# Layer norms of a two-block kernel: from VectorE's subtract-and-multiply to a row shift on VectorE and a scale-and-bias on ScalarE

## The chip, the cores and the metric

One core of a Trainium2 chip runs the kernel. The core has five engines, each with its own instruction queue worked off in order: PE (TensorE), DVE (VectorE), ACT (ScalarE), POOL (GpSimd) and SP (SyncE, which here only starts DMAs). They wait for each other through semaphores. The metric is the device time of one launch in microseconds, lower is better; the kernel before takes 7072.08 us in the median of 3 runs (7069.32 to 7072.81).

## The reference

A batch of 32 sequences of 256 tokens with 128 channels goes through two residual blocks. Cut to what matters:

```
_layernorm(x) = (x - mean(x)) / sqrt(var(x) + 1e-5)        # per token, over 128 channels

x = x + A(_layernorm(x))          # A: q, k, v with causal conv and silu, rope, a gated delta rule
                                  #    over 16 heads of 64, output gate, Wo
x = x + F(_layernorm(x)), where F(y):
    h = LN(y) * g1 + b1;  y = y + softmax_attention(h) @ Wo
    m = LN(y) * g2 + b2;  y + top-2-of-8 experts(m)
```

So there are four layer norms for each sequence: one of the input (`xn`), one of the first block's result (`xf`), one of `xf` again (`hn` for attention) and one of `x2`, the state behind attention (`hn` again, for the experts). Each is 256 tokens, held as two tiles of 128 tokens (partitions) by 128 channels.

## The kernel before

All five engines run the same software pipeline of turns. In turn i, `back` works on sequence i (the delta rule: heads, a blocked triangular inverse, state), `front` on sequence i+1 (norm, projections, conv, rope), `V` on i (values), `attn` on i-1 (output gate, second block's norms and attention, router) and `experts` on i-2. There are turns -1 to 32; turns 3 to 29 are one hardware loop. A hand-written table `SIDE` says after which milestone of `back` each engine takes which step of the other streams. A step that an engine has no part in costs it nothing, and each engine keeps to the table's order, so a step that waits holds up all that stands behind it on its engine.

The layer norms stand at these places:

- `front stat` at "start" and `front xln` at ("head", 2): statistics of `xin`, then `xn`. PE turns `xn` over at ("head", 3), step `xT`, ahead of expert step `up 1` and the next pair of heads. ACT's place at ("head", 2) lies behind `silu 0` and `silu 1` of the attention stream, which need POOL's `normalise`.
- `attn stat` and `attn xf` at ("head", 11): `x1` becomes `xf`, and the statistics of `xf` follow at once. `gate 0` of the front stands between them.
- `attn hT` at "kT": `xf` becomes `hn`, PE turns it over, ACT copies it to `hT` with g1 and b1.
- `attn fWo` at ("o", 0) has the statistics of `x2`; `attn mT` at "end" makes `hn`, PE turns it over, ACT copies it to `mT` with g2 and b2, and the router follows.

Each norm is made so: DVE takes bn_stats and bn_aggr (mean and variance in `mv` or `fmv`) and adds eps (`ln_stats`, L1408 to L1416); POOL raises the variance to -1/2 (`rstd` L711, `frstd` L789); DVE then makes `(x - mean) * rstd` by one tensor_scalar for each of the two tiles (`ln_apply`, L1421). `v_ln` and `f_ln` are the semaphores that count these DVE steps, 5 for each norm. POOL's `normalise` (L721, L723) multiplies the delta rule's output of one token tile, 128x1024, in two instructions; its second tile is done in the next turn at ("head", 1), its first in "cross" 1.

Of the kernel before, what the change touches and what calls it, by code (L numbers as in the profile page):

```python
# [27 lines left out]
ALU = mybir.AluOpType  # L28
# [3 lines left out]
P = 128  # L32
# [182 lines left out]
def program(nc, a, out):  # L215
# [3 lines left out]
    with ExitStack() as ctx:  # L219
        def sb(name, shape, dt=F32):  # L220
            return ctx.enter_context(nc.sbuf_tensor(name, shape, dt))
# [46 lines left out]
        def bank(use):  # L268
            return banks[bank_of[use]]
# [190 lines left out]
        x1_ready = signal("x1_ready", 1)  # L460
        v_ln = signal("v_ln", 5)
        p_rstd = signal("p_rstd", 1)
# [45 lines left out]
        a_yT = signal("a_yT", 4)  # L508
        f_ln = signal("f_ln", 15)
        fp_rstd = signal("fp_rstd", 3)  # L510
# [124 lines left out]
        def _(sp):  # L635
# [19 lines left out]
            def one(i):  # L655
# [21 lines left out]
                if ahead is not None and not (last and ahead == B - 1):  # L677
                    hold(v_ln.sem, v_ln.at(ahead, 5))
                    sp.dma_start(xin[:], x_rows(i[0] + 2 if isinstance(i, tuple) else ahead + 1)).then_inc(x_in.sem, 16)
# [15 lines left out]
        def _(pool):  # L695
# [87 lines left out]
            def attn(j, step, n):  # L783

                if step == "norm":
                    normalise(j, 1)
                elif step in ("stat", "xf", "fWo"):
                    pool.wait_ge(f_ln.sem, f_ln.at(j, {"stat": 3, "xf": 8, "fWo": 13}[step]))
                    g.tensor_tensor(frstd[:], fmv[:, :, 1], neg_half[:, 0:1].to_broadcast([P, NT]),  # L789
                                    ALU.pow).then_inc(fp_rstd.sem, 1)  # L790
                elif step == "b2":

                    g.tensor_tensor(x1[:], x1[:], x2[:], ALU.add).then_inc(p_xs.sem, 1)
# [35 lines left out]
        def _(act):  # L829
# [36 lines left out]
            def values(i, step, m):  # L866
# [17 lines left out]
                elif step == "copy":  # L884
                    act.wait_ge(*full_at(i, ("vT", m)))
                    if m == 0 and begun(i, 0):
                        act.wait_ge(v_y.sem, v_y.at(i, 0))
                    s.copy(V[:, :, 4 * m:4 * m + 4, :],  # L888
                           bank(("vT", m))[:].rearrange("p (t h d) -> p t h d", t=NT, h=4)).then_inc(a_V.sem, 1)

            def front(k, step, n):
                if step == "xT":
                    act.wait_ge(*full_at(k, "xT"))
# [85 lines left out]
            def attn(j, step, n):  # L979
# [55 lines left out]
        def _(pe):  # L1035
# [54 lines left out]
            def front(k, step, n):  # L1090
                if step == "xT":
                    pe.wait_ge(v_ln.sem, v_ln.at(k, 5))
                    wait_free(pe, "xT")
# [166 lines left out]
            def attn(j, step, n):  # L1260
# [20 lines left out]
                elif step == "hT":  # L1281
                    pe.wait_ge(f_ln.sem, f_ln.at(j, 10))
                    for t in range(NT):
# [66 lines left out]
                elif step == "mT":  # L1350
                    pe.wait_ge(f_ln.sem, f_ln.at(j, 15))
                    for t in range(NT):
# [44 lines left out]
        def _(dve):  # L1397
# [19 lines left out]

            def ln_apply(i, x_, mv_, rs, out_, sig, rsig, rk):
                dve.wait_ge(rsig.sem, rsig.at(i, rk))
                for t in range(NT):  # L1420
                    v.tensor_scalar(out_[:, t, :], x_[:, t, :], mv_[:, t, 0:1], rs[:, t:t + 1], ALU.subtract,  # L1421
                                    ALU.mult).then_inc(sig.sem, 1)

# [95 lines left out]
            def front(k, step, n):  # L1519
# [3 lines left out]
                elif step == "xln":  # L1523
                    ln_apply(k, xin, mv, rstd, xn, v_ln, p_rstd, 1)
                elif step == "gate" and n == 0:
# [121 lines left out]
            def attn(j, step, n):  # L1647
# [12 lines left out]
                elif step == "xf":  # L1660
                    ln_apply(j, x1, fmv, frstd, xf, f_ln, fp_rstd, 1)
                    dve.wait_ge(f_ln.sem, f_ln.at(j, 5))
                    ln_stats(j, xf, fstats, fmv, f_ln, 5)
                elif step == "hT":
                    ln_apply(j, xf, fmv, frstd, hn, f_ln, fp_rstd, 2)
                elif step == "fqk":
# [43 lines left out]
                elif step == "fWo":  # L1710
# [126 lines left out]
```

## Time and profile before

| | |
|---|---|
| median of 3 runs | 7072.08 us |
| profiled execution, first to last instruction | 7067.6 us |
| PE busy | 5137.7 us (73%) |
| DVE busy | 4870.4 us (69%) |
| ACT busy | 3485.1 us (49%) |
| POOL busy | 2615.7 us (37%) |
| chain that ended last | PE 41%, issue 23%, DVE 19%, ACT 10%, POOL 6% |

The profile page gives for the profiled execution its span, from the first to the last instruction; the median of the timed runs lies 4.5 us above it, which is what lies around the span. No engine is busy all the time: the table says what each engine had to do, the chain says whose work the end waited for, and here it goes back and forth between engines, so where an instruction stands in its turn matters more than how much its engine has to do.

### The profile page before, as it was taken

To read this page: it belongs to the slowest core of one execution; us is meant where nothing else is said; L and a number is where in the kernel's file an instruction comes from. 1 tells how busy PE (TensorE), PEld (TensorE's weight loads), DVE (VectorE), ACT (ScalarE), POOL (GpSimd) and SP (SyncE) were. 2 spreads that over 40 slices of the span, in tenths; PEclk is the share of its full clock that TensorE was granted. 3 is DMA by queue.
4 is the path that set the end of the run, shared out by engine and by line. 5 is a ranking of instruction groups with operands and counts; after the bars stand their busy time and mean duration, and the time that the engine had idled before them with its cause. 6 is when DMAs were issued, how large, how long until landed. Compare 5 with 4: busy or idle time off the path is not lost.

```text
span 7067.6 us, 126933 instructions
## 1 busy us (share of the span) xinstructions
PE 5137.7 (73%) x40448; PEld 3663.3 (52%) x40448; DVE 4870.4 (69%) x11585; ACT 3485.1 (49%) x5995; POOL 2615.7 (37%) x2957
## 2 busy tenths in 40 slices
PE   3677777777767777777777677777777777777776
PEld 2455555555545555555555455555455454555555
DVE  5667777667776677776677776677766777767752
ACT  2345554545554545545555545455444555455533
POOL 3444333344333444333443334343333433334420
PEclk6677877777877878777778778777777787777777
DMA  1000010000010100110000101000100001000001
GB/s 47 8 20 25 24 34 30 28 26 27 27 34 27 31 22 24 34 34 24 28 25 27 34 27 31 25 28 26 34 27 28 25 24 34 30 28 28 25 25 44
DMA packets 214675, 199.48 MB, mean 28 GB/s; under 512 B 13848, under 2 KB 176416, under 8 KB 209696
## 3 DMA queue, kind: packets, MB, share of 16 engines
q1 hardware_dynamic: 213920, 190.01, 8.9%
q8 instruction: 401, 6.57, 0.4%
q14 instruction: 354, 2.90, 0.1%
HBM read 148.02 MB, written 4.19 MB: 22 GB/s over the span
## 4 chain that ended last, share of the span: by engine, by line
PE 41%; issue 23%; DVE 19%; ACT 10%; POOL 6%; DVEq 1%; ACTq 0%; DMA 0%; SPq 0%; POOLq 0%
PE bank L1039 38%; DVE acc L1433 3%; PE bank L1043 3%; DVE NP L1575 3%; DVE tmpb L1602 2%; DVE mx L1684 2%; DVE Gam L1566 2%; ACT acc L854 2%; POOL fo L716 1%; ACT h L1026 1%; ACT L883 1%; POOL QK L816 1%; POOL nrm L728 1%; DVE Gam L1605 1%; ACT acc L877 1%
## 5 line engine op out<-in xcount | busy, mean ns | idle before, releaser
L1039 PE MATMUL bank<-QK 64*128 64x256 f32 (+1 forms) x4096 | 858.2, 427 | 628.9 <-DVE NP L1575 298.3
L1433 DVE SCALAR_TENSOR_TENSOR acc<-bank,conv_w,acc 128x255 f32<-128x255 f32 (+2 forms) x2304 | 931.8, 473 | 379.7 <-ACT acc L854 197.5
L1039 PEld LDWEIGHTS bank<-QK 64*128 64x128 f32 (+1 forms) x4096 | 358.1, 173 | 1059.4 <-issue 378.1
L1026 ACT ACTIVATE h<-bank,b 128x256 f32<-128x256 f32 x1024 | 415.8, 473 | 611.2 <-PE bank L1039 607.5
L854 ACT ACTIVATE acc<-bank,conv_b,conv_w 128x256 f32<-128x256 f32 x512 | 260.8, 559 | 868.6 <-PE bank L1039 716.3
L1039 PE MATMUL bank<-mT,W 128*128 128x256 f32 x2048 | 665.5, 483 | 24.4 <-DMA W<-in_W 22.6
L789 POOL TENSOR_TENSOR frstd<-fmv,neg_half 128x2 f32<-128x2 f32 x96 | 66.8, 696 | 1350.7 <-DVE fmv L1416 1350.7
L1039 PEld LDWEIGHTS bank<-mT,W 128*128 128x128 f32 x2048 | 502.2, 255 | 121.1 <-DMA W<-in_W 24.1
L1039 PE MATMUL bank<-W,h 128*128 128x128 f32 x4096 | 515.7, 280 | 55.4 <-DVE QK L1701 51.4
L810 POOL TENSOR_TENSOR sq<-acc 128x256 f32<-128x256 f32 x256 | 186.4, 728 | 973.7 <-ACT acc L860 973.7
L1039 PEld LDWEIGHTS bank<-W,h 128*128 128x128 f32 x4096 | 490.9, 194 | 105.6 <-DVE QK L1701 63.0
L1566 DVE TENSOR_TENSOR_SCAN Gam<-bank,ident_pad 128x258 f32<-128x258 f32 x512 | 351.8, 687 | 272.5 <-PE bank L1039 272.5
L746 POOL TENSOR_TENSOR Gam<-Gam 128x80 f32<-128x80 f32 (+11 forms) x736 | 272.3, 370 | 549.3 <-DVE Gam L1597 501.5
L924 ACT COPY Gam<-NP 32x256 f32<-32x256 f32 x512 | 321.6, 628 | 306.3 <-DVE fac L1582 301.8
L818 POOL TENSOR_TENSOR rot<-rot,sin 128x512 f32<-128x512 f32 x256 | 384.2, 1501 | 153.6 <-DVE rot L1549 153.6
L1039 PE MATMUL bank<-xnT,Wqkv 128*128 128x256 f32 x1024 | 381.1, 508 | 72.1 <-DVE acc L1433 71.9
L1575 DVE SCALAR_TENSOR_TENSOR NP<-bank,es,Gam 128x256 f32<-128x256 f32 x1024 | 432.9, 466 | 0.0
L1605 DVE TENSOR_TENSOR Gam<-Gam,tmpb 128x112 f32<-128x112 f32 (+29 forms) x992 | 368.3, 371 | 38.8 <-DVE tmpb L1602 5.7
L800 POOL TENSOR_TENSOR V<-V,nrm 128x1024 f32<-128x1024 f32 x64 | 121.4, 1918 | 735.1 <-ACT V L888 735.1
L1684 DVE TENSOR_REDUCE mx<-bank 128x2 f32<-128x512 f32 x512 | 319.7, 679 | 80.5 <-PE bank L1039 80.5
L1602 DVE TENSOR_TENSOR tmpb<-Gam 128x112 f32<-128x112 f32 (+29 forms) x992 | 352.7, 356 | 23.4
L1002 ACT ACTIVATE pT<-bank 128x512 f32<-128x512 f32 x512 | 281.8, 596 | 90.5 <-PE bank L1039 89.6
(227 smaller groups left out, 11769.9 us busy)
## 6 DMA issues: line engine op xcount, KB each, us to landing
W<-in_W SPq DMA_DIRECT2D x512, 256.0 KB, 2.9
QK<-QK SPq DMA_DIRECT2D x32, 1024.0 KB, 5.4
xin<-in_x SPq DMA_DIRECT2D x32, 128.0 KB, 2.2
x<-in_x SPq DMA_DIRECT2D x32, 128.0 KB, 2.2
xnG<-xnT SPq DMA_DIRECT2D x32, 128.0 KB, 2.0
out<-moe SPq DMA_DIRECT2D x32, 128.0 KB, 2.0
NP<-in_c_alpha_sel SPq DMA_DIRECT2D x1, 1024.0 KB, 5.0
Wqkv<-in_Wq SPq DMA_DIRECT2D x1, 512.0 KB, 6.1
```

Of the source, the lines that this page charges most:

```text
L818: g.tensor_tensor(rot[:, b], rot[:, b], sin[:].unsqueeze(1).to_broadcast([P, 2, T]), ALU.mult).then_inc(p_rope.sem, 1)
L854: ins = s.activation(acc[:, n % 2, kind, :], ps[:, kind, :], ACT.Identity, bias=conv_b[:, kind, n:n + 1], scale=conv_w[:, kind, n, PAD:KT])
L924: ins = s.copy(Dg[ROWS[q]].rearrange("p k (t h) -> p k t h", t=NT)[:, :, :, heads - 4:heads], units[:, :, :, heads - 4:heads])
L1002: s.activation(pT[:, n % 4], pair(bank(("st", n))), ACT.Exp, scale=float(FD) ** -0.5)\
L1026: ins = s.activation(h1[:, n % 2, f, :], ps[:, q, :], ACT.Gelu_apprx_tanh, bias=b1[:, n, f:f + 1])
L1039: return mm(out_, lhsT, rhs, start=first, stop=last)
L1433: v.scalar_tensor_tensor(acc[:, n % 2, m, j:T], ps[:, m, 0:T - j], conv_w[:, kind, c, PAD - j:KT - j], acc[:, n % 2, m, j:T], ALU.mult, AL ...
L1566: v.tensor_tensor_scan(Gam[:, h, :], ps[:, 0:NT * GW], ident_pad[:], 0.0, ALU.mult, ALU.add)\
L1575: ins = v.scalar_tensor_tensor(NP[:, t * H + h - 1, :, :], ps[:, t * T:(t + 1) * T].rearrange("p (a k) -> p a k", a=2), es[:, t, h - 1:h], ...
L1602: v.tensor_tensor(tmp_, Eb[:, r + 1:, r:r + 1].to_broadcast([P, n, w]), X[:, r:r + 1, 0:w].to_broadcast([P, n, w]), ALU.mult).then_inc(v_b ...
L1605: v.tensor_tensor(X[:, r + 1:, 0:w], X[:, r + 1:, 0:w], tmp_, ALU.subtract).then_inc(v_blk.sem, 1)
L1684: v.tensor_reduce(mx[:, :, n], ps, AX.X, ALU.max).then_inc(v_mx.sem, 1)
```

## The change

The two tiles' subtract-and-multiply leaves DVE. In its place DVE makes one small tensor of two columns, `shift = -mean * rstd` (one scalar_tensor_tensor of 128x2), and ACT makes `x * rstd + shift`, one activation (Identity, scale and bias from columns) for each tile. Who needs the result waits for new semaphores of ACT, `a_xn` (1 a sequence) and `a_fln` (3 a sequence): PE before each of the three transposes, SP before it loads the next `xin`, and DVE itself before the statistics of `xf`. `v_ln` now counts 4 and `f_ln` 12 steps.

```diff
-            def ln_apply(i, x_, mv_, rs, out_, sig, rsig, rk):
+            def ln_shift(i, mv_, rs, shift_, sig, rsig, rk):
+
                 dve.wait_ge(rsig.sem, rsig.at(i, rk))
-                for t in range(NT):
-                    v.tensor_scalar(out_[:, t, :], x_[:, t, :], mv_[:, t, 0:1], rs[:, t:t + 1], ALU.subtract,
-                                    ALU.mult).then_inc(sig.sem, 1)
+                v.scalar_tensor_tensor(shift_[:], mv_[:, :, 0], -1.0, rs[:], ALU.mult, ALU.mult).then_inc(sig.sem, 1)
...
+            def apply(out_, x_, rs, shift_, done):
+
+                for t in range(NT):
+                    ins = s.activation(out_[:, t, :], x_[:, t, :], ACT.Identity, bias=shift_[:, t:t + 1],
+                                       scale=rs[:, t:t + 1])
+                ins.then_inc(done.sem, 1)
+
             def front(k, step, n):
-                if step == "xT":
+                if step == "xln":
+                    act.wait_ge(v_ln.sem, v_ln.at(k, 4))
+                    apply(xn, xin, rstd, shift, a_xn)
+                elif step == "xT":
...
+                elif step == "xf":
+                    act.wait_ge(f_ln.sem, f_ln.at(j, 4))
+                    apply(xf, x1, frstd, fshift, a_fln)
                 elif step == "hT":
+                    act.wait_ge(f_ln.sem, f_ln.at(j, 8))
+                    apply(hn, xf, frstd, fshift, a_fln)
                     act.wait_ge(*full_at(j, "hT"))
...
                 elif step == "mT":
+                    act.wait_ge(f_ln.sem, f_ln.at(j, 12))
+                    apply(hn, x2, frstd, fshift, a_fln)
                     act.wait_ge(*full_at(j, "mT"))
...
                 if step == "xT":
-                    pe.wait_ge(v_ln.sem, v_ln.at(k, 5))
+                    pe.wait_ge(a_xn.sem, a_xn.at(k, 1))
...
                 elif step == "hT":
-                    pe.wait_ge(f_ln.sem, f_ln.at(j, 10))
+                    pe.wait_ge(a_fln.sem, a_fln.at(j, 2))
...
                 elif step == "mT":
-                    pe.wait_ge(f_ln.sem, f_ln.at(j, 15))
+                    pe.wait_ge(a_fln.sem, a_fln.at(j, 3))
...
                 elif step == "xf":
-                    ln_apply(j, x1, fmv, frstd, xf, f_ln, fp_rstd, 1)
-                    dve.wait_ge(f_ln.sem, f_ln.at(j, 5))
-                    ln_stats(j, xf, fstats, fmv, f_ln, 5)
+                    ln_shift(j, fmv, frstd, fshift, f_ln, fp_rstd, 1)
+                    dve.wait_ge(a_fln.sem, a_fln.at(j, 1))
+                    ln_stats(j, xf, fstats, fmv, f_ln, 4)
```

The other calls of `ln_apply` (steps `xln`, `hT` and `mT`) become `ln_shift` in the same way, and POOL's three waits for `f_ln` count 3, 7 and 11 in place of 3, 8 and 13.

On ACT, in the hardware loop from "end" over the loop's branch to ("head", 3), the order before is this (L1011 is the copy to `mT`, L1026 the experts' gelu, L982 `silu 0` and `silu 1`, L896 the copy of the turned `xn`):

```order
L1011 ACTIVATE mT<-bank,ln_gb 128x256
L1015 ACT_TABLE_LOAD
L1015 ACTIVATE ex<-lg 128x16
L910 COPY sumsT<-bank 96x256
L557 REGISTER_ALU
L557 COMPARE_AND_BRANCH
L1026 ACT_TABLE_LOAD
L1026 ACTIVATE h<-bank,b 128x256 x4
L982 ACT_TABLE_LOAD
L982 ACTIVATE Gam<-Gam 128x1024
L982 ACTIVATE Kt<-Kt 128x1024
L896 COPY xnT<-bank 128x256
```

The same place now (lines are numbered anew: L898 is `apply`, L996 the two silu):

```order
L898 ACTIVATE hn<-x,fshift,frstd 128x128 x2
L1031 REGISTER_ALU
L1032 ACTIVATE mT<-bank,ln_gb 128x256
L1036 ACT_TABLE_LOAD
...
L1047 ACTIVATE h<-bank,b 128x256 x4
L996 ACT_TABLE_LOAD
L996 ACTIVATE Gam<-Gam 128x1024
L996 ACTIVATE Kt<-Kt 128x1024
L898 ACTIVATE xn<-xin,shift,rstd 128x128 x2
L910 COPY xnT<-bank 128x256
```

The pair of `hn` stands directly ahead of the copy to `mT`, the pair of `xn` behind both silu; no table load has come in.

On DVE at ("head", 11), the order before, from the end of `gate 0` (L1533) over `xf` and its statistics to the experts' sum (L1766):

```order
L1533 TENSOR_SCALAR zmin<-z 128x32
L1421 TENSOR_SCALAR xf<-x,fmv,frstd 128x128 x2
L1408 BN_STATS fstats<-xf 128x6 x2
L1413 BN_AGGR fmv<-fstats 128x2 x2
L1416 TENSOR_SCALAR fmv<-fmv 128x2
L1766 SCALAR_TENSOR_TENSOR moe<-bank,wsel,moe 128x128 x2
```

And now (L1442 is `ln_shift`):

```order
L1553 TENSOR_SCALAR zmin<-z 128x32
L1442 SCALAR_TENSOR_TENSOR fshift<-fmv,frstd 128x2
L1429 BN_STATS fstats<-xf 128x6 x2
L1434 BN_AGGR fmv<-fstats 128x2 x2
L1437 TENSOR_SCALAR fmv<-fmv 128x2
L1786 SCALAR_TENSOR_TENSOR moe<-bank,wsel,moe 128x128 x2
```

Between the shift and the statistics DVE now waits for ACT, and the experts' sum and the next head stand behind that wait.

## Rows read from the trace of the kernel before

**Rows 1.** Groups of instructions on DVE, forms apart: xcount | busy us, mean ns | idle.
```profile
L1421 DVE TENSOR_SCALAR hn<-x,fmv,frstd 128x128 f32<-128x128 f32 x64 | 135.9, 2163 | 0.8 <-POOL frstd L789 0.8
L1421 DVE TENSOR_SCALAR xn<-xin,mv,rstd 128x128 f32<-128x128 f32 x64 | 131.3, 2092 | 9.2 <-POOL rstd L711 9.0
```

**Rows 2.** Timeline at "end" of one turn: start us, us, engine, line, op.
```profile
3027.87 1.19 DVE L1515 TENSOR_SCALAR ms<-ms 128x16 f32<-128x16 f32 x1
3028.97 4.41 DVE L1421 TENSOR_SCALAR hn<-x,fmv,frstd 128x128 f32<-128x128 f32 x2
3028.99 1.90 POOL L721 TENSOR_TENSOR Gam<-Gam,fo 128x1024 f32<-128x1024 f32 x1
3030.96 2.34 POOL L723 TENSOR_TENSOR Gam<-Gam,onorm 128x1024 f32<-128x1024 f32 x1
3033.30 0.71 DVE L1552 TENSOR_TENSOR QK<-QK,rot 128x512 f32<-128x512 f32 x1
3033.53 0.66 PE L1043 MATMUL bank<-ident,hn 128*128 128x128 f32 x2 [5.85 <-DVE hn L1421]
3034.23 0.56 ACT L1011 ACTIVATE mT<-bank,ln_gb 128x256 f32<-128x256 f32 x1 [5.92 <-PE bank L1043]
```

**Rows 3.** Source line L1512, a scalar_tensor_tensor with two SBUF inputs: ns min/median/max.
```profile
L1512 DVE SCALAR_TENSOR_TENSOR ms<-sk,ms x64: 174/410/1427, 251.7 to 6877.6; 128x16 f32<-128x16 f32 x64
```

**Rows 4.** Groups of instructions on ACT, forms apart.
```profile
L854 ACT ACTIVATE acc<-bank,conv_b,conv_w 128x256 f32<-128x256 f32 x512 | 260.8, 559 | 868.6 <-PE bank L1039 716.3 <-DVE rot L1549 101.0 <-POOL QK L816 45.1
...
L896 ACT COPY xnT<-bank 128x256 f32<-128x256 f32 x32 | 11.8, 368 | 26.8 <-PE bank L1043 26.8
...
L833 ACT CAST identb<-ident 128x128 bf16<-128x128 f32 x1 | 0.3, 298 | 15.6 <-DMA NP<-in_c_k_sel 15.6
```

**Rows 5.** Timeline at ("head", 2) and ("head", 3) of one turn.
```profile
3051.32 1.90 POOL L721 TENSOR_TENSOR Kt<-Kt,fo 128x1024 f32<-128x1024 f32 x1
3051.38 4.34 DVE L1421 TENSOR_SCALAR xn<-xin,mv,rstd 128x128 f32<-128x128 f32 x2 [0.17 <-POOL rstd L711]
3053.29 2.35 POOL L723 TENSOR_TENSOR Kt<-Kt,onorm 128x1024 f32<-128x1024 f32 x1
3053.75 1.28 ACT L982 ACT_TABLE_LOAD   x1
...
3056.00 1.04 ACT L982 ACTIVATE Kt<-Kt 128x1024 f32<-128x1024 f32 x1
3056.38 0.39 PE L1039 MATMUL bank<-alpha,alpha_sel 128*128 128x258 bf16 x1 [2.25 <-DVE Gam L1566]
3056.74 0.69 PE L1043 MATMUL bank<-ident,xn 128*128 128x128 f32 x2
...
3061.46 0.69 DVE L1566 TENSOR_TENSOR_SCAN Gam<-bank,ident_pad 128x258 f32<-128x258 f32 x1 [2.93 <-PE bank L1039]
```

**Rows 6.** Timeline at ("head", 11) of the same turn.
```profile
3091.87 0.21 ACT L900 ACTIVATE emin<-zmin 128x32 f32<-128x32 f32 x1
3091.98 0.60 DVE L1421 TENSOR_SCALAR xf<-x,fmv,frstd 128x128 f32<-128x128 f32 x2 [0.30 <-POOL frstd L789]
...
3092.62 0.49 DVE L1408 BATCH_NORM_STATS2 fstats<-xf 128x6 f32<-128x128 f32 x2
...
3093.90 0.61 DVE L1766 SCALAR_TENSOR_TENSOR moe<-bank,wsel,moe 128x128 f32<-128x128 f32 x2 [0.19 <-PE bank L1039]
```

**Rows 7.** Timeline at "kT" and ("block", 0) of the same turn.
```profile
3108.92 2.54 ACT L924 COPY Gam<-NP 32x256 f32<-32x256 f32 x4
...
3110.20 0.59 DVE L1421 TENSOR_SCALAR hn<-xf,fmv,frstd 128x128 f32<-128x128 f32 x2
3110.85 0.44 PE L1043 MATMUL bank<-ident,hn 128*128 128x128 f32 x2 [1.43 <-DVE hn L1421]
...
3112.40 1.02 ACT L877 ACTIVATE acc<-bank,conv_b,conv_w 128x256 f32<-128x256 f32 x2 [0.35 <-PE bank L1039]
...
3113.53 0.87 DVE L1433 SCALAR_TENSOR_TENSOR acc<-bank,conv_w,acc 128x255 f32<-128x255 f32 x2 [0.20 <-ACT acc L877]
```

More of the change, by code:

```diff
@@ L339, in program @@
         rstd = sb("rstd", [P, NT])
+        shift = sb("shift", [P, NT])
         xn = sb("xn", [P, NT, HID])
@@ L408, in program @@
         frstd = sb("frstd", [P, NT])
+        fshift = sb("fshift", [P, NT])
         xf = sb("xf", [P, NT, HID])
@@ L460, in program @@
         x1_ready = signal("x1_ready", 1)
-        v_ln = signal("v_ln", 5)
+        v_ln = signal("v_ln", 4)
+        a_xn = signal("a_xn", 1)
         p_rstd = signal("p_rstd", 1)
@@ L508, in program @@
         a_yT = signal("a_yT", 4)
-        f_ln = signal("f_ln", 15)
+        f_ln = signal("f_ln", 12)
+        a_fln = signal("a_fln", 3)
         fp_rstd = signal("fp_rstd", 3)
@@ L677, in one @@
                 if ahead is not None and not (last and ahead == B - 1):
-                    hold(v_ln.sem, v_ln.at(ahead, 5))
+                    hold(a_xn.sem, a_xn.at(ahead, 1))
                     sp.dma_start(xin[:], x_rows(i[0] + 2 if isinstance(i, tuple) else ahead + 1)).then_inc(x_in.sem, 16)
@@ L787, in attn @@
                 elif step in ("stat", "xf", "fWo"):
-                    pool.wait_ge(f_ln.sem, f_ln.at(j, {"stat": 3, "xf": 8, "fWo": 13}[step]))
+                    pool.wait_ge(f_ln.sem, f_ln.at(j, {"stat": 3, "xf": 7, "fWo": 11}[step]))
                     g.tensor_tensor(frstd[:], fmv[:, :, 1], neg_half[:, 0:1].to_broadcast([P, NT]),
@@ L1523, in front @@
                 elif step == "xln":
-                    ln_apply(k, xin, mv, rstd, xn, v_ln, p_rstd, 1)
+                    ln_shift(k, mv, rstd, shift, v_ln, p_rstd, 1)
                 elif step == "gate" and n == 0:
@@ L1660, in attn @@
                 elif step == "xf":
-                    ln_apply(j, x1, fmv, frstd, xf, f_ln, fp_rstd, 1)
-                    dve.wait_ge(f_ln.sem, f_ln.at(j, 5))
-                    ln_stats(j, xf, fstats, fmv, f_ln, 5)
+                    ln_shift(j, fmv, frstd, fshift, f_ln, fp_rstd, 1)
+                    dve.wait_ge(a_fln.sem, a_fln.at(j, 1))
+                    ln_stats(j, xf, fstats, fmv, f_ln, 4)
                 elif step == "hT":
-                    ln_apply(j, xf, fmv, frstd, hn, f_ln, fp_rstd, 2)
+                    ln_shift(j, fmv, frstd, fshift, f_ln, fp_rstd, 2)
                 elif step == "fqk":
@@ L1715, in attn @@
                     dve.wait_ge(v_x2.sem, v_x2.at(j, 1))
-                    ln_stats(j, x2, fstats, fmv, f_ln, 10)
+                    ln_stats(j, x2, fstats, fmv, f_ln, 8)
                 elif step == "mT":
-                    ln_apply(j, x2, fmv, frstd, hn, f_ln, fp_rstd, 3)
+                    ln_shift(j, fmv, frstd, fshift, f_ln, fp_rstd, 3)
                 elif step == "router":
```

## The prediction

> **What bounds the kernel now.** I read the page first: no engine is full, and the chain that ended last changes engine all the time (PE 41%, DVE 19%, ACT 10%). So the busy time taken from DVE says little by itself; what counts is at which place of a turn who is waited for. Second, the groups by form. Two of the four norms' instructions are very dear: a 128x128 tensor_scalar takes 2163 ns for `hn` ahead of the experts and 2092 ns for `xn` [rows 1], while the same operation at the other two places takes 0.59 and 0.60 us for both tiles [rows 6, 7]. Third, the timeline of one turn of the loop at each of the four places, with all engines.
>
> It shows why the two are dear. At "end" the pair of `hn` starts at 3028.97 and ends at 3033.38; POOL's two `normalise` instructions fill 3028.99 to 3033.30 [rows 2]. At ("head", 2) the pair of `xn` lasts from 3051.38 to 3055.72, POOL's pair from 3051.32 to 3055.64 [rows 5]. DVE stands still while POOL multiplies: each of its tiles gets through at the end of one POOL instruction. At ("head", 11) and "kT" POOL does nothing of the kind.
>
> **The price of the new instructions.** *ACT's pair.* No row shows Identity on 128x128 out of SBUF with two column operands. A plain copy of 128x128 takes 298 ns; at 128x256 two column operands (L854, 559) cost 191 ns more than a copy (L896, 368) [rows 4]. I take 298 + 191 = 489 ns for one. L877, the same form as L854, takes 1.02 us for two [rows 7], 0.10 less than 2 x 0.559, so the pair is 0.88 us. Bounds: 0.50 (two of 298, overlapped) and 1.02 (two of 128x256). ACT's order has no new table load.
>
> *DVE's shift.* Nearest is L1512, the same operation with two SBUF inputs and 16 columns: 174 ns at best, median 410, up to 1427 [rows 3]. I take 0.17 us where POOL is quiet. At the two places beside `normalise` I take it to be held like the instruction that it replaces, until the POOL instruction that runs ends, then 0.17. Bounds: 0.17 (not held), or held over both POOL instructions.
> By the Trainium skill (SBUF — State Buffer, "Who interferes with whom") a VectorE instruction with two SBUF inputs, or in a two-port mode, contends with a GpSimd instruction that reads SBUF, and the later one blocks fully; the shift has two SBUF inputs. The spread of L1512 agrees, the shift itself is in no row.
>
> **The change place by place** (the turn shown; what is later or earlier in it than before):
>
> *"end", `mT`.* L1515 ends at 3029.06, with POOL's L721 just begun [rows 2]. The shift is held until 3030.89 and is done at 3031.06; it takes one POOL instruction's wait where `hn` took two. ACT is idle there (5.92 us before L1011), so its pair runs 3031.10 to 3031.98 and PE transposes at 3032.04 in place of 3033.53: 1.5 us earlier. The copy to `mT`, the router's softmax and the rest of the turn hang on it one behind another. DVE's L1552 stands behind the shift and is now held by L723 alone, to about 3033.8 (before 3034.01), still ahead of the router's first reduction. **-1.5 us.**
>
> *("head", 2) and 3, `xn`.* DVE gets free at about 3053.4 in place of 3055.72, and the decay matmul that waited 2.25 us for its scan [rows 5] starts over a microsecond sooner. But PE's next instruction is the transpose of `xn`, and that now waits for ACT, which stands in its own queue: experts' gelu, a table load of 1.28 us at 3053.75, both silu, the second to 3057.04 [rows 5]. Only then the pair: to 3057.87. PE transposes at 3057.93 in place of 3056.74. Behind it on PE are `up 1`, the next pair of heads and their decays, and DVE waits for those (2.93 us at 3061.46, released by PE [rows 5]), so that DVE's gain is spent in waiting and the delay goes on to all. **+1.2 us.**
>
> *("head", 11), `xf`.* The shift ends at 3092.15 and ACT is through with `emin` at 3092.08 [rows 6]; pair to 3093.07, about 0.1 us for the semaphore, so the statistics start at 3093.2 in place of 3092.62. The experts' sum had waited 0.19 us for PE anyway [rows 6]: **+0.4 us.** Queued behind DVE's wait are that sum, a scan and the head's products, for which PE waits next. ACT's next gelu is 0.9 us late, but it had some 1 us to spare.
>
> *"kT", `hT`.* Nothing is held by POOL here. DVE's pair ended at 3110.79; now the shift is done at 3110.4, but ACT is copying the diagonal blocks to 3111.46 [rows 7], so its pair ends at about 3112.3 and PE transposes at 3112.35 in place of 3110.85. Behind that on PE stands the values' projection, then ACT's first tap (before 3112.40), then DVE's taps (3113.53, waiting 0.20 for ACT) [rows 7]: all **+1.5 us**. DVE gains 0.4 us and waits it off at its next instruction, the transpose that needs the diagonal blocks.
>
> Busy time taken from DVE is 135.9 + 131.3 us [rows 1] and 32 times the 0.60 and 0.59 us of the other two, less 128 shifts. I give nothing for it beyond the above: at each place the engine behind it is waited for. I looked in the rest of the turn for a wait that ends by something not delayed (a DMA, POOL) and could swallow the sum, and found none: every releaser itself hangs on DVE or PE.
>
> **The sum.** The two busy places occur where a `back` and an `attn` both run: `mT` 31 times, `xn` behind silu 30 times, `xf` and `hT` 31 times. 30 x 1.2 = 36, 31 x 0.4 = 12, 31 x 1.5 = 46, 31 x (-1.5) = -46; together **+48 us**. The first turns (`xn` without silu) and the last add about 1 us. Span 7067.6 + 49 = 7117; with the 4.5 us between span and median **7121 us**, 0.7% more than 7072.08.
>
> The bounds of ACT's pair move each of four places by -0.38 or +0.14, or -47 and +17 us in all. The shift not held at "end" gives 1.9 us a turn more, -57.
>
> **Rivals.**
>
> *A, the shift gets through at once.* For: L1512 has runs of 174 ns, and the shift is so small that it may slip in between two POOL instructions. Against: L1515, one small input, took 1.19 us right before [rows 2]. At "end" the gain is 3.4 us a turn, at ("head", 2) nothing changes since ACT is late anyway. 7121 - 57 = 7064, about the time of before.
>
> *B, the delays at "kT" and ("head", 2) are hidden and the gain at "end" is not.* Then 7072 - 46 + 12 = 7038, faster. It needs slack of 1.5 us on PE and ACT together; at "kT" DVE waits only 0.20 us for ACT's tap [rows 7], so the slack would have to lie later in the turn.
> By the Trainium skill (ScalarE: Activation LUTs, "Rules for kernel authors") adding and multiplying belong on VectorE. At "kT", where POOL is quiet, the trace has 0.59 us for DVE's pair against my 0.88 for ACT's, which agrees in size; but more than the pair's length it is ACT's queue that costs here.
>
> *C, much slower: the shift is held over both POOL instructions.* DVE's next chance at "end" comes after L723: shift at 3033.4, pair to 3034.3, PE 0.8 us later than before in place of 1.5 earlier. 31 x 2.3 = 71 more: 7192. For: `hn`'s second tile was held through all of L723 [rows 2]. Against: its first tile got in between, as L1515 did before.
>
> *D, the work removed counts in full*, as it would if DVE bounded the kernel: 267 us less [rows 1], some 6810. The waits of DVE for PE and ACT at each place speak against it.
>
> **How the numbers follow.** The forecast's mechanism has 0.73 (its own range, by the price of ACT's pair and 0.3 us a place, 7075 to 7150), A 0.12, B with D 0.10, C 0.05. A measurement of this kernel tells about 0.2%, 14 us, from no change: 7058 to 7086. A falls mostly inside it, the low end of the forecast too. Faster 0.13, same 0.17, slower 0.70. Range 7060 to 7155: it takes in A and the bounds of ACT's pair, and leaves out B, D and C.
>
> **What the profile of the changed kernel would show.** ACT's pair 0.88 us for two; the shift 0.17 us at ("head", 11) and "kT", about 2 us at "end" and ("head", 2). PE's transpose of `xn` released by ACT about 1 us behind the second silu's end; DVE idle 0.9 to 1.0 us ahead of the statistics of `xf`, released by ACT; PE idle about 3 us before the transpose of `hn` at "kT", and about 4.3 in place of 5.85 us at "end". A turn of the loop would take 1.6 us more. I am wrong if the shift at "end" takes 0.2 us (A), or if a turn is not longer though all four places moved as said (B).

## The result and the profile after

The changed kernel takes **7098.73 us** (median of 4 runs, 7094.27 to 7106.99), the kernel before 7070.91 us beside it on the same chip: ratio 1.0041, 95% interval 1.003 to 1.0053. That is 28 us slower, 0.4%. The forecast was 7121 us, 49 above 7072.08. The sign came out as forecast. Of the four places the mechanism held whole at two (`xn` and `xf`); at "end" and "kT" it held in part, and two errors that partly cancel brought the sum near.

| | before | after |
|---|---|---|
| span of the profiled execution | 7067.6 us | 7094.7 us |
| PE busy | 5137.7 us | 5153.1 us |
| DVE busy | 4870.4 us | 4701.6 us |
| ACT busy | 3485.1 us | 3594.9 us |
| POOL busy | 2615.7 us | 2622.5 us |

DVE has 169 us less to do and the kernel is slower. In the chain that ended last, the time in which an engine waited for nothing that the profile shows ("issue") has grown from 23 to 34%. PE's share has shrunk from 41 to 30% and DVE's from 19 to 16%, while ACT's and POOL's have grown a little (10 to 11, 6 to 8):

```profile
issue 34%; PE 30%; DVE 16%; ACT 11%; POOL 8%; DVEq 0%; ACTq 0%; DMA 0%; SPq 0%; POOLq 0%
```

The new instructions in the groups of the changed kernel, ACT and then DVE (xcount | busy us, mean ns | idle before them), which stand where [rows 1] stood:

```profile
L898 ACT ACTIVATE hn<-x,fshift,frstd 128x128 f32<-128x128 f32 x64 | 28.1, 485 | 46.9 <-DVE fshift L1442 46.9
...
L898 ACT ACTIVATE xn<-xin,shift,rstd 128x128 f32<-128x128 f32 x64 | 27.6, 478 | 11.1 <-DVE shift L1442 11.1
```

```profile
L1442 DVE SCALAR_TENSOR_TENSOR shift<-mv,rstd 128x2 f32<-128x2 f32 x32 | 55.9, 1746 | 9.4 <-POOL rstd L715 9.3
...
L1442 DVE SCALAR_TENSOR_TENSOR fshift<-fmv,frstd 128x2 f32<-128x2 f32 x96 | 31.7, 330 | 11.6 <-POOL frstd L793 11.6
```

ACT's instruction takes 485 ns (489 forecast). The shift, which has two numbers for each row, takes 1746 ns in the mean at ("head", 2).

**"end", `mT`.** The timeline of the changed kernel, in answer to [rows 2]:

```profile
3260.98 1.18 DVE L1535 TENSOR_SCALAR ms<-ms 128x16 f32<-128x16 f32 x1
3262.08 0.15 DVE L1442 SCALAR_TENSOR_TENSOR fshift<-fmv,frstd 128x2 f32<-128x2 f32 x1
3262.08 1.91 POOL L725 TENSOR_TENSOR Gam<-Gam,fo 128x1024 f32<-128x1024 f32 x1
3262.16 2.38 DVE L1572 TENSOR_TENSOR QK<-QK,rot 128x512 f32<-128x512 f32 x1
3262.26 0.88 ACT L898 ACTIVATE hn<-x,fshift,frstd 128x128 f32<-128x128 f32 x2 [0.84 <-DVE fshift L1442]
...
3263.28 0.41 PE L1064 MATMUL bank<-ident,hn 128*128 128x128 f32 x2 [2.49 <-ACT hn L898]
```

Shift and POOL's L725 start at the same hundredth of a microsecond, and the shift is through in 0.15 us; the one that is held is now DVE's L1572 behind it (2.38 us; as L1552 in [rows 2] it took 0.71). PE waits 2.49 us where it waited 5.85. A turn earlier it goes the other way:

```profile
3043.04 1.93 DVE L1442 SCALAR_TENSOR_TENSOR fshift<-fmv,frstd 128x2 f32<-128x2 f32 x1
3043.06 1.90 POOL L725 TENSOR_TENSOR Gam<-Gam,fo 128x1024 f32<-128x1024 f32 x1
...
3046.03 0.66 PE L1064 MATMUL bank<-ident,hn 128*128 128x128 f32 x2 [4.27 <-ACT hn L898]
```

This is the turn that I had forecast (shift 2 us, PE waiting 4.3). But of the 31 turns with a `back` beside it the shift is through in 0.15 us in 22, held for 1.93 us in 8 and for 2.31 us in one. In the 30 turns of the first two kinds the trace has the shift's start 0 to 0.017 us ahead of L725's, so the recorded order does not tell which of the two is held. In the kernel before, the 128x128 instruction of `hn` started 0.002 to 0.019 us ahead of L721 and was held for 1.99 us in all 30.

**("head", 2) and 3, `xn`.** In answer to [rows 5]:

```profile
3064.16 1.90 POOL L725 TENSOR_TENSOR Kt<-Kt,fo 128x1024 f32<-128x1024 f32 x1
3064.22 1.85 DVE L1442 SCALAR_TENSOR_TENSOR shift<-mv,rstd 128x2 f32<-128x2 f32 x1 [0.16 <-POOL rstd L715]
...
3066.84 1.28 ACT L996 ACT_TABLE_LOAD   x1
...
3069.10 1.04 ACT L996 ACTIVATE Kt<-Kt 128x1024 f32<-128x1024 f32 x1
3070.04 0.86 ACT L898 ACTIVATE xn<-xin,shift,rstd 128x128 f32<-128x128 f32 x2
...
3071.04 0.69 PE L1064 MATMUL bank<-ident,xn 128*128 128x128 f32 x2 [2.50 <-ACT xn L898]
...
3077.22 0.69 DVE L1586 TENSOR_TENSOR_SCAN Gam<-bank,ident_pad 128x258 f32<-128x258 f32 x1 [6.81 <-PE bank L1060]
```

DVE starts its shift 0.06 us behind POOL's multiplication and is held by it, in all 30 turns; it is free at 3066.07, and yet the transposition waits until ACT has loaded its table and done both silu: 0.90 us behind the second silu's end. What DVE has won it waits off at the scan (6.81 us, before 2.93).

**("head", 11), `xf`.** In answer to [rows 6]:

```profile
3106.69 0.21 ACT L914 ACTIVATE emin<-zmin 128x32 f32<-128x32 f32 x1
3106.79 0.16 DVE L1442 SCALAR_TENSOR_TENSOR fshift<-fmv,frstd 128x2 f32<-128x2 f32 x1 [0.30 <-POOL frstd L793]
3106.99 0.88 ACT L898 ACTIVATE xf<-x,fshift,frstd 128x128 f32<-128x128 f32 x2
3107.90 0.48 DVE L1429 BATCH_NORM_STATS2 fstats<-xf 128x6 f32<-128x128 f32 x2 [0.94 <-ACT xf L898]
```

The statistics start 1.21 us behind `emin` in place of 0.75.

**"kT", `hT`.** In answer to [rows 7]:

```profile
3125.46 2.51 ACT L938 COPY Gam<-NP 32x256 f32<-32x256 f32 x4
3126.38 0.15 DVE L1442 SCALAR_TENSOR_TENSOR fshift<-fmv,frstd 128x2 f32<-128x2 f32 x1
...
3128.00 0.88 ACT L898 ACTIVATE hn<-xf,fshift,frstd 128x128 f32<-128x128 f32 x2
...
3128.93 0.69 PE L1064 MATMUL bank<-ident,hn 128*128 128x128 f32 x2 [3.36 <-ACT hn L898]
...
3129.41 1.91 PE L1060 MATMUL bank<-xnG,Wqkv 128*128 128x256 f32 x4
...
3131.57 1.02 ACT L881 ACTIVATE acc<-bank,conv_b,conv_w 128x256 f32<-128x256 f32 x2 [1.35 <-PE bank L1060]
```

The shift waits for nothing, and ACT reads it 1.5 us later, behind its block copies. From the start of those copies to the transposition it is 3.47 us, before 1.93; to the first tap 6.11 us, before 3.48. The surplus over the forecast 1.5 us has a cause that I had not reckoned with. The values' projection takes 1.91 us now; in the turn of [rows 7] the timeline of the kernel before has

```profile
3111.12 1.03 PE L1039 MATMUL bank<-xnG,Wqkv 128*128 128x256 f32 x4
```

so PE does the same four matmuls at about half the speed behind its longer wait: the granted clock over the 1.91 us is 0.50, over the 1.03 us of before 1.00.

**The whole turn.** The table has what the parts of a turn last, in us, in means over turns 4 to 27, with the granted clock of TensorE behind the stroke (2.4 GHz is 1.00, 1.2 GHz is 0.50). The last five columns are kernels in which only the norms named are made in the new way; they are described under the experiments. The rows run from the start of `back` to the transposition of `xn`, to ACT's gate, to the transposition of the diagonal blocks, to the first tap, to the cast of q and k, to the attention's first maximum, then a stretch up to the statistics of `ms`, then to the router's maximum at "end", then the rest:

| | before | after | mT alone | xn alone | hT alone | hT + mT | xn + mT |
|---|---|---|---|---|---|---|---|
| to xn's transposition | 11.82 / .64 | 13.21 / .65 | 11.76 / .62 | 13.16 / .67 | 11.81 / .61 | 11.77 / .63 | 13.24 / .65 |
| to the gate | 34.33 / .82 | 34.83 / .80 | 33.56 / .83 | 34.47 / .82 | 33.18 / .85 | 33.47 / .83 | 35.06 / .80 |
| to the blocks | 20.75 / .91 | 21.33 / .89 | 20.67 / .92 | 21.61 / .89 | 20.83 / .92 | 21.74 / .89 | 21.29 / .88 |
| to the first tap | 1.90 / 1.00 | 3.96 / .75 | 1.91 / 1.00 | 1.76 / 1.00 | 3.77 / .82 | 4.03 / .76 | 1.82 / 1.00 |
| to the cast | 7.12 / 1.00 | 7.12 / .91 | 7.12 / 1.00 | 7.12 / 1.00 | 7.12 / .92 | 7.12 / .94 | 7.12 / 1.00 |
| to the first maximum | 15.30 / .53 | 13.62 / .67 | 15.44 / .52 | 14.78 / .57 | 13.27 / .69 | 13.74 / .66 | 14.49 / .60 |
| to the statistics of ms | 104.81 | 105.73 | 105.54 | 105.34 | 106.16 | 105.84 | 105.34 |
| to the router's maximum | 10.26 / .79 | 7.03 / .89 | 6.77 / .92 | 10.26 / .77 | 10.19 / .75 | 6.83 / .89 | 7.74 / .88 |
| rest | 8.71 / .50 | 9.24 / .50 | 9.28 / .50 | 8.72 / .50 | 8.69 / .50 | 9.23 / .50 | 9.21 / .50 |
| turn | 215.00 | 216.08 | 212.06 | 217.22 | 215.04 | 213.78 | 215.31 |

After against before: 1.4 us lost at `xn`, 2.1 at "kT", 3.2 won at "end", and 1.7 won between the cast and the first maximum, where nothing was changed. The other stretches lose 2.5 us together, and the turn is 1.08 us longer.

### The profile page after: what moved, and what is told of

Read it like the earlier page. It is cut to its first block, busy times and chain, and to the rows that moved or that the text cites. A ratio compares the mean times of both kernels' runs of the same rounds, so it can differ in the third digit from the quotient of the medians.

```text
span 7094.7 us, 127116 instructions
## 1 busy us (share of the span) xinstructions
PE 5153.1 (73%) x40448; PEld 3691.9 (52%) x40448; DVE 4701.6 (66%) x11457; ACT 3594.9 (51%) x6251; POOL 2622.5 (37%) x2957
## 4 chain that ended last, share of the span: by engine, by line
issue 34%; PE 30%; DVE 16%; ACT 11%; POOL 8%; DVEq 0%; ACTq 0%; DMA 0%; SPq 0%; POOLq 0%
PE bank L1060 28%; DVE acc L1453 4%; DVE tmpb L1622 2%; DVE mx L1704 2%; PE bank L1064 2%; ACT acc L858 2%; ACT h L1047 1%; POOL fo L720 1%; DVE NP L1595 1%; POOL QK L820 1%; DVE Gam L1625 1%; ACT Gam L938 1%; POOL Kt L727 1%; POOL nrm L732 1%; DVE Gam L1629 1%
## 5 line engine op out<-in xcount | busy, mean ns | idle before, releaser
L1060 PE MATMUL bank<-QK 64*128 64x256 f32 (+1 forms) x4096 | 882.7, 441 | 640.5 <-DVE NP L1595 308.9
L1060 PE MATMUL bank<-mT,W 128*128 128x256 f32 x2048 | 688.5, 496 | 24.9 <-DMA W<-in_W 23.1
L1060 PE MATMUL bank<-W,h 128*128 128x128 f32 x4096 | 543.5, 289 | 49.4 <-DVE QK L1721 48.1
L1060 PEld LDWEIGHTS bank<-W,h 128*128 128x128 f32 x4096 | 520.9, 203 | 93.5 <-DVE QK L1721 59.7
L1622 DVE TENSOR_TENSOR tmpb<-Gam 128x112 f32<-128x112 f32 (+29 forms) x992 | 356.3, 359 | 21.1
L1060 PEld LDWEIGHTS bank<-Gam,NP 32*32 32x32 f32 (+1 forms) x6144 | 314.2, 154 | 34.0 <-issue 34.0
```

Of the source, the lines that this page charges most:

```text
L1060: return mm(out_, lhsT, rhs, start=first, stop=last)
L1622: v.tensor_tensor(tmp_, Eb[:, r + 1:, r:r + 1].to_broadcast([P, n, w]), X[:, r:r + 1, 0:w].to_broadcast([P, n, w]), ALU.mult).then_inc(v_b ...
```

## The experiments

All kernels below but one ("What holds DVE") have a switch. It says which of the four norms are made in the new way; the others stay as before, with the counts of `v_ln` and `f_ln` to match.

```diff
+ON_ACT = ('mT',)
...
                 elif step == "mT":
+                    if "mT" in ON_ACT:
+                        act.wait_ge(f_ln.sem, f_ln.at(j, LN["mT"]))
+                        apply(hn, x2, frstd, fshift, a_fln)
                     act.wait_ge(*full_at(j, "mT"))
```

**One norm at a time.** The first four runs, timed beside the kernel before (7070.07 us), differ in this line alone, the first having `('mT',)`:

```diff
-ON_ACT = ('mT',)
+ON_ACT = ('xn',)      # the second; ('hT',) the third, ('xf',) the fourth
```

> Only the norm at 'end' (step mT) is shift on VectorE and scale-and-shift on ScalarE; the other three stay on VectorE. Theory (each place adds its own part): the transpose of hn comes 1.6 us earlier in turns where the shift is held by POOL's L721-type instruction and about 3.7 us earlier where it gets through, as in the changed kernel, so 2.8 to 3.3 us a turn, 31 turns: 85 to 105 us less, about 6975. Rival 1 (what I forecast, shift always held): 1.5 us a turn, 46 us less, 7025. Rival 2 (the gain at 'end' is swallowed by the start of the next turn): within 15 us of before.

Measured: 6981.06 us, ratio 0.9881 [0.9865, 0.9898], **89 us faster**. My own theory had it 95 faster on the strength of the trace after; the forecast's -1.5 us a turn (46 us in all) is refuted. The shift is through at once in 23 turns and held for 1.93 us in 7.

> Only the norm of the input (step xln) is changed. Theory: PE's transpose of xn waits for ScalarE's two silu and the pair of applies and comes 1.4 us later than before in each of 30 turns; all of it goes on to the end of the turn: 40 to 60 us more, about 7120. Rival (VectorE's gain of 2.4 us at this place counts, since the kernel is short of VectorE): 30 to 70 us less, about 7020.

Measured: 7133.77 us, 1.0091 [1.0074, 1.0107], **64 us slower**. The place itself costs 1.34 us a turn (table, first row), near the 1.2 forecast; another 0.9 us is lost ahead of the diagonal blocks.

> Only the norm at 'kT' (step hT) is changed. Theory as forecast: transpose of hn 1.4 to 1.5 us later, all of it kept, 31 turns: 46 us more, about 7117. Rival (what the stage table of the changed kernel suggests: the blocks stage behind it gets shorter by 1.3 us of the 1.7): about 0.4 us a turn, 12 us more, about 7083.

Measured: 7069.93 us, 1.0002 [0.9992, 1.0011], **no change**, though the stretch to the first tap is 1.9 us longer in the mean and at least 1.6 us in every turn. The forecast's +46 us falls, and so do the 12 us of the rival. Where it comes back is seen in stretches of the same turn (us, busy of PE, PEld, DVE, ACT, POOL, then the granted clock), before and with `hT` alone:

```profile
3113.53:3120.64 7.11, 3.87 (x22) 2.71 (x20) 6.60 (x18) 3.84 (x6) 5.86 (x17) 1.00 0.27 74
3120.64:3136.36 15.72, 12.62 (x64) 8.42 (x64) 12.14 (x33) 8.26 (x21) 2.10 (x5) 0.50 0.01 2
```

```profile
3111.74:3115.37 3.63, 2.71 (x13) 2.50 (x14) 1.66 (x3) 2.44 (x6) 1.75 (x7) 0.77 0.00 0
3115.37:3122.49 7.12, 5.14 (x26) 4.10 (x25) 6.84 (x18) 3.85 (x6) 6.02 (x15) 0.88 0.27 74
3122.49:3135.98 13.49, 10.39 (x64) 6.96 (x64) 11.60 (x32) 8.26 (x21) 0.49 (x2) 0.68 0.00 1
```

Before, PE runs at full clock up to the cast and then does 64 matmuls, for which DVE waits, wholly at 1.2 GHz, in 12.62 us. With `hT` on ACT the lower clock begins already while PE waits and during the taps, where DVE is the busy engine (6.84 of 7.12 us) and a slow PE costs nothing: that stretch stays 7.12 us long. Of the 64 matmuls a part then runs at 2.4 GHz, and all together take 10.39 us. From the blocks to the first maximum it is 24.3 us in the mean before and 24.2 with `hT` alone.

Is it the clock? In this turn the stretch is 2.23 us shorter, and PE's busy time in it falls by 2.23 us. In all 216 turns of the nine kernels measured so, the stretch lasts PE's busy time and 3.09 to 3.10 us more. POOL's tail beside these matmuls is shorter with `hT` alone too (2.10 to 0.49 us), but that is not it, as the kernel before shows by itself. In four of its 24 turns the clock falls otherwise, without any edit; one of them:

```profile
4197.90:4211.43 13.53, 10.43 (x64) 6.99 (x64) 11.72 (x33) 8.26 (x21) 2.74 (x5) 0.68 0.00 1
```

There POOL's tail is longer (2.74 us), and the stretch is as short as with `hT` alone. Those four turns win 2.2 us here and lose 1.6 us ahead of the blocks, at a clock of 0.85 for 0.92, and 0.7 us up to the gate: in sum they are no shorter than the others.

> Only the norm at head 11 (step xf) is changed. Theory: statistics of xf start 0.5 us later, and 0.4 us of it reach the end of the turn: 12 us more, about 7083. Rival: the new wait of VectorE for ScalarE shifts later work out of step with PE and costs over 1 us a turn: over 30 us more.

Measured: 7075.71 us, 1.0011 [1.0002, 1.0021], 6 us slower. The interval is 1 to 15 us, so the forecast 12 stands.

The four together make -20 us, the changed kernel measured +28 against the kernel before. So 48 us lie in their company, which the pairs below look into. The intervals of the single times are 7 to 12 us to either side, so the 48 are known to some 20.

**`xn` ahead of the silu.** The step `xln` changes place with the two silu; only ACT notices, since DVE has no part in the silu.

```diff
-    (("head", 2), steps("attn", ("silu", 0), ("silu", 1)) + steps("front", ("xln", 0))),
+    (("head", 2), steps("front", ("xln", 0)) + steps("attn", ("silu", 0), ("silu", 1))),
```

> Only the norm of the input is changed, as in the run with xn alone, and the table puts the step xln ahead of silu 0 and silu 1 at head 2, so that ScalarE makes xn before its table load and both silu. Theory (the loss at this place was ScalarE's queue, not ScalarE): xn is ready 2.3 us sooner than behind the silu, PE's transpose no longer waits for it and comes at least 1.0 us earlier than in the kernel before: 20 to 50 us less than before, about 7035, and some 95 us less than xn alone. Rival (the loss is the longer way over two engines, wherever it stands in the queue): still 40 us or more above before, 7110 or more. Rival 2: the silu, now 0.9 us later, hold up the output gate: within 15 us of before.

Measured: 7024.12 us, 0.9936 [0.9919, 0.9952], **46 us faster** than before and 110 us faster than `xn` alone behind the silu (the kernel before, here and in the next three: 7069.69 us). The timeline of this kernel at ("head", 2):

```profile
3031.05 1.85 DVE L1487 SCALAR_TENSOR_TENSOR shift<-mv,rstd 128x2 f32<-128x2 f32 x1 [0.16 <-POOL rstd L741]
...
3033.54 0.87 ACT L924 ACTIVATE xn<-xin,shift,rstd 128x128 f32<-128x128 f32 x2
3034.43 1.28 ACT L1023 ACT_TABLE_LOAD   x1
...
3036.00 0.44 PE L1094 MATMUL bank<-ident,xn 128*128 128x128 f32 x2
```

ACT makes `xn` at 3033.54, ahead of the table load, and PE's transposition waits for nobody. The same work on the same engine costs 64 us or earns 46 by its place in the queue.

**What holds DVE.** In the kernel before, POOL's two multiplications are cut to the first of 16 heads; the output lacks the rest of `normalise`, so this time is only for the mechanism.

```diff
-                g.tensor_tensor(O[t], O[t], bc(fo[:, t, :], DH), ALU.mult).then_inc(p_on.sem, 1)
+                g.tensor_tensor(O[t][:, 0:1], O[t][:, 0:1], bc(fo[:, t, 0:1], DH), ALU.mult).then_inc(p_on.sem, 1)
```

> The kernel before, with the two normalise instructions of GpSimd working on one head of 16 (128x64 in place of 128x1024), so that the other heads' outputs aren't scaled by their norm and onorm_w; nothing else is changed. Theory (VectorE's tensor_scalar is held as long as GpSimd's multiplication runs, and not slow by itself): the pairs of xn and hn at head 2 and 'end' fall from 4.34 and 4.41 us to 0.6 to 1.1 us, and the turn gets 3 to 5 us shorter: 90 to 150 us less, about 6950. Rival (those two are slow for another reason, such as their buffers or the clock of that stage): they stay above 3.5 us and the time stays within 30 us of before.

Measured: 6900.99 us, 0.9763 [0.9747, 0.9779]. DVE's groups, to be held against [rows 1]:

```profile
L1421 DVE TENSOR_SCALAR hn<-x,fmv,frstd 128x128 f32<-128x128 f32 x64 | 25.1, 431 | 0.8 <-POOL frstd L789 0.8
L1421 DVE TENSOR_SCALAR xn<-xin,mv,rstd 128x128 f32<-128x128 f32 x64 | 22.4, 392 | 8.7 <-POOL rstd L711 8.5
```

Each of POOL's multiplications takes 0.29 to 0.33 us here, and the same DVE instructions take 431 and 392 ns in place of 2163 and 2092. POOL's multiplication was what held them, and 169 us of the kernel hang on it, more than the 90 to 150 expected (POOL's own work, which is shorter too, is in that number, so it is no pure price of the hold).

**Another place for the experts' norm.** If POOL's multiplication is the price at "end", the norm can be made ahead of it, and on DVE as before. The statistics of `x2` are there since ("o", 0); a new step `norm2` at ("top", 1) makes `hn`, and `mT` keeps the transposition alone.

```diff
     (("o", 0), steps("attn", ("fWo", 0))),
+    (("top", 1), steps("attn", ("norm2", 0))),
     (("cross", 1), steps("front", ("silu", 7))),
```

> No norm on ScalarE: all four are VectorE's subtract-and-multiply as before; only the one for the experts is taken at top 1, right behind its statistics, where GpSimd does not multiply yet, in place of at 'end'. Theory (at 'end' what counts is when hn is ready, not which engine makes it): the pair takes about 0.6 us, PE transposes hn as soon as its own matmuls are done, 5 to 6 us earlier than before: 120 to 180 us less, about 6920, and below the run with this norm alone on ScalarE (6981). Rival (GpSimd's multiplications at 'end' then hold the next VectorE instructions, so that little is left): 60 us less or under.

Measured: 6958.35 us, 0.9838 [0.9821, 0.9854], **111 us faster**, 38 short of what I expected. The hold has found others, as the timeline of this kernel shows:

```profile
3205.15 1.91 POOL L752 TENSOR_TENSOR Gam<-Gam,fo 128x1024 f32<-128x1024 f32 x1
3205.24 2.37 DVE L1622 TENSOR_TENSOR QK<-QK,rot 128x512 f32<-128x512 f32 x1
...
3208.18 1.77 DVE L1811 TENSOR_TENSOR gt<-ex 128x128 f32<-128x128 f32 x1 [0.28 <-ACT ex L1068]
```

L1622 takes 2.37 us for 0.71 in [rows 2] (there L1552), and the router's comparison L1811 is held too, in the groups of this kernel and of the kernel before:

```profile
L1811 DVE TENSOR_TENSOR gt<-ex 128x128 f32<-128x128 f32 x32 | 55.2, 1726 | 9.0 <-ACT ex L1068 9.0
```

```profile
L1731 DVE TENSOR_TENSOR gt<-ex 128x128 f32<-128x128 f32 x32 | 9.4, 294 | 9.0 <-ACT ex L1015 9.0
```

The router comes earlier now, and so under POOL's second multiplication.

The next one has this and `xn` on ACT ahead of the silu.

```diff
-ON_ACT = ()
+ON_ACT = ('xn',)
...
-    (("head", 2), steps("attn", ("silu", 0), ("silu", 1)) + steps("front", ("xln", 0))),
+    (("head", 2), steps("front", ("xln", 0)) + steps("attn", ("silu", 0), ("silu", 1))),
```

> The two together: the norm for the experts early on VectorE, the norm of the input on ScalarE ahead of the silu, the other two on VectorE as before. Theory: their gains add up, about 7070 - 150 - 35 = 6885, below both kernels. Rival: TensorE's slower clock after the removed waits takes back half: about 6980.

Measured: 6924.94 us, 0.9799 [0.9782, 0.9815], 145 us faster; the two apart have 111 and 46, so they all but add up. It is 40 us above the 6885 that I expected, since the first of the two had fallen short already.

**Pairs and the whole.** The last four run beside 7071.68 us of the kernel before.

```diff
+ON_ACT = ('xn', 'mT')                  # first; table SIDE as before
+ON_ACT = ('hT', 'mT')                  # second; table SIDE as before
+ON_ACT = ('xn', 'xf', 'hT', 'mT')      # third; xln ahead of the silu
+ON_ACT = ('xn', 'mT')                  # fourth; xln ahead of the silu, norm2 at ("top", 1)
```

> The norms of the input and at 'end' are changed, in their old places; xf and hT stay on VectorE. Theory (parts add up as measured alone: +64 and -89): 25 us less than before, about 7045. Rival (the changed kernel's parts don't add up, alone they give -20 and together +28, and it is these two that collide): 20 us or more above before, about 7090.

Measured: 7067.59 us, 0.9994 [0.9984, 1.0003]: 4 us faster, where the two apart give 25; neither the theory nor the rival had that. One difference of the size of the missing 21 us stands at "end", in the shift. The line of its source, for `mT` alone and for the pair (ns min/median/max):

```profile
L1487 DVE SCALAR_TENSOR_TENSOR fshift<-fmv,frstd x32: 147/148/2303, 455.5 to 6901.9; 128x2 f32<-128x2 f32 x32
```

```profile
L1487 DVE SCALAR_TENSOR_TENSOR fshift<-fmv,frstd x32: 147/1928/2305, 454.8 to 6999.3; 128x2 f32<-128x2 f32 x32
```

With `xn` on ACT too, the shift is held for 1.93 us in 18 turns in place of 7: 11 x 1.78 us = 20 us. That this is the cause is argued, not shown. The counts are of one execution each, for `mT` alone of the fastest of four (6968 us, the median 6981). And against what the two apart would give in sum, the pair loses 0.97 us a turn up to the router's maximum, but 1.35 us up to the gate too, and is about 1.3 us better over the other stretches.

> The norms at 'kT' and 'end' are changed, in their old places. Alone the one at 'kT' cost nothing, since the spell of TensorE's slower clock behind it began while TensorE waited for ScalarE, and alone the other gave -89. Theory (the free delay at 'kT' hangs on where the slower clock falls, and a turn that is shorter elsewhere moves that): 20 to 45 us above the run with mT alone, about 7010. Rival (it stays free): within 12 us of 6981.

Measured: 7038.35 us, 0.9965 [0.9951, 0.9979]: 33 us faster, and so **56 us slower than `mT` alone**, though `hT` alone cost nothing, and more than the 20 to 45 us expected. Here the race at "end" is no cause (22 turns through, 8 held, nearly as for `mT` alone). The table has it in the stretches: against `mT` alone the pair loses 2.12 us to the first tap, gets 1.70 back up to the first maximum, and loses 1.07 us more ahead of the blocks, at a granted clock of 0.89 for 0.92. `hT` alone had won 1.15 us up to the gate (clock 0.85 for 0.82) and lost 1.35 in the long stretch behind the first maximum; `mT` alone wins 0.77 in the first of these by itself, and the pair does not win it twice. A loss ahead of the blocks at a lower clock is also what the four odd turns of the kernel before had.

> The changed kernel with the step xln ahead of silu 0 and silu 1 in the table; nothing else. Theory (the loss of xn is ScalarE's queue also with all four changed): some 100 us less than the changed kernel's 7099, about 6995, clearly faster than before. Rival (the other three hold the turn up so that xn's place counts little): within 40 us of 7099.

Measured: 6957.94 us, 0.9847 [0.9831, 0.9864]: all four norms on ACT, **114 us faster than before and 141 faster than the changed kernel**, by the one line of the table `SIDE`. That is more than the 100 us which I expected of it.

> As the fastest so far (the norm for the experts early at top 1, the norm of the input on ScalarE ahead of the silu; 6925), but the norm for the experts by shift and ScalarE's pair in place of VectorE's subtract-and-multiply. Theory (what counts is only that hn is ready by 'end'): within 15 us of 6925. Rival (ScalarE's pair is waited for at top 1, where it stands ahead of silu 7): 30 us or more above it.

Measured: **6910.82 us**, 0.9778 [0.9761, 0.9794], the fastest that computes everything, and 14 us below the same kernel with this norm on DVE, as the theory had it (within 15). Its timeline at ("top", 1):

```profile
3583.88 1.90 POOL L799 TENSOR_TENSOR Gam<-V,dd 128x1024 f32<-128x1024 f32 x1
...
3585.19 0.61 DVE L1489 SCALAR_TENSOR_TENSOR fshift<-fmv,frstd 128x2 f32<-128x2 f32 x1
...
3585.83 0.88 ACT L925 ACTIVATE hn<-x,fshift,frstd 128x128 f32<-128x128 f32 x2 [1.76 <-DVE fshift L1489]
```

Here another of POOL's multiplications runs, and the shift gets through at its end (3585.78), after 0.61 us.

## Why the prediction was right in sign and off in size

**What bounds the kernel: right.** Taking 169 us from DVE gave nothing in itself; every engine behind it was waited for (rival D falls, but see below what the hold was worth).

**Price of ACT's pair: right.** 0.88 us forecast, 0.88 and 0.86 measured, and 0.88 at "end" beside POOL's multiplication.

**`xn`, +1.2 us a turn: right at its place, too small for the kernel.** The transposition came 1.34 to 1.4 us late by the table. `xln` ahead of the silu turned it to -46 us, so ACT's queue was the cause of the loss, as argued. Alone it cost 64 us over 30 turns, 2.1 us each: the term was mis-sized by what follows later in the turn.

**The shift held: right at ("head", 2), wrong at "end".** The sentence "The shift is held until 3030.89" places it at L1515's end, 0.07 us behind POOL's start. In truth DVE's next instruction starts 0.1 us ahead of that end, as `hn` did in [rows 2], and so within 0.02 us of POOL's in 30 turns of 31. The 128x128 tile was held from such a start in all 30 turns; the 128x2 gets through in 22. Rival A was therefore true in 22 turns of this place, and the forecast's mechanism in 8. With 1.78 us more in 22 turns the term is -46 - 39 = -85 us, an estimate; `mT` alone measured -89.
By the Trainium skill (SBUF — State Buffer, "Who interferes with whom") a VectorE instruction with two SBUF inputs and a GpSimd one that reads SBUF exclude each other and the later one waits. The runs agree where the order is clear, down to 128x2: started 0.06 us behind POOL's multiplication, the shift took 1.85 us in 30 turns of 30. With starts within 0.02 us the recorded order does not settle it: ahead by 0 to 0.017 us, the shift was through in 22 turns and held in 8. And not every GpSimd instruction that reads SBUF holds VectorE so. In the turn of [rows 2], POOL's raising to a power runs from 3033.26 to 3036.15, and DVE's L1552 beside it, with two SBUF inputs, takes 0.71 us:

```profile
3033.26 2.89 POOL L716 TENSOR_TENSOR fo<-ms,neg_half 128x16 f32<-128x16 f32 x1
```

**`xf`, +0.4 us: right at its place** (0.46 us), and not refuted in its sum (6 us measured, interval 1 to 15, for 12).

**`hT`, +1.5 us: its place right, its effect on the end wrong.** The delay to the first tap is 1.9 us, but alone it moved the kernel by nothing. I had looked for "a wait that ends by something not delayed" and found none; what gave the time back was no wait. The spell at the lower clock moved, and the 64 matmuls that DVE waits for took 10.39 us of PE in place of 12.62. The forecast kept PE's speed as it was. Rival B, hidden delay at "kT", was true of `hT` alone; in the company of `mT` it cost 56 us.

**The sum.** The forecast has -46 + 36 + 12 + 46 = +48. The four apart measure -89 + 64 + 6 + 0 = -20, and what they do to each other adds 48 more. The pair `xn` and `mT` is 21 us worse than its parts, which more held shifts at "end" may explain, and the pair `hT` and `mT` 56. These two pairs alone would overshoot the 48, so the company does not add up pair by pair either. That the forecast is only 20 us from the result is luck, two errors that partly cancel: its terms are 67 us too dear in sum (`mT` 43, `hT` 46, `xf` 6, against `xn` 28 too cheap), and the interplay of 48 us is missing. The 1.08 us by which a turn got longer (1.6 forecast) are not the four delays of the forecast added up.

**What stays open.** In the stretch up to the first maximum the clock is the cause of the time won, by the 3.09 to 3.10 us that the stretch has beside PE's busy time in every turn and by the four turns of the kernel before. What made the lower clock fall elsewhere in those four, and why the delay at `hT` does it in every turn, no run here shows. Nor is it shown why the other stretches with `hT` alone (1.15 us won up to the gate, 1.35 lost behind the first maximum) come out even. The 56 us of `hT` beside `mT` are placed in the turn, with the clock that goes with them, but not explained further, and what decides whether the shift at "end" is held is open too.

## What to carry to other kernels

When an elementwise step moves to another engine, look first at what stands ahead of it in that engine's queue: a table load and two activations made the difference between 64 us lost and 46 won. Ask why the old instruction was slow: here it was five times its own length because of POOL's multiplication beside it, and a tiny instruction with two SBUF inputs can inherit that hold whole. Moving the norm in time won 111 us, moving it to another engine 89. Effects of single edits read from stages need not add up (-20 us apart, +28 together); run them together.

## What the runs showed of the hardware that I had not expected

- A DVE instruction on 128x2 is held as long as POOL's multiplication beside it lasts, like one on 128x128: 1.85 us at ("head", 2), 1.93 and 2.31 us at "end", 0.15 us without the hold.
- Where POOL and DVE start within 0.02 us of each other, the 128x2 shift was held in 8 turns of 30 though its start is never recorded behind POOL's; the 128x128 tensor_scalar of before was held in all 30. Where the shift got through in the turn shown, L1572 behind it was held (2.38 us for 0.71).
- A spell at 1.2 GHz can move with a wait of PE that is some 2 us longer, onto work that does not mind it: with `hT` delayed, the granted clock of the 64 matmuls ahead of the first maximum rose from 0.50 to 0.68 in the turn shown. In four of 24 turns of the kernel before it had done so by itself, and cost as much elsewhere.
